# Normalising attention's output with features on partitions, its rows gathered by transfers

## The reference

```python
x = x + 0.5 * _L0_ffn_ref(_layernorm(x), ...)      # 8 experts, every token through each
x = x + _L0_attn_ref(_layernorm(x), ...)
x = x + 0.5 * _L0_ffn_ref(_layernorm(x), ...)
...
attn = jax.nn.softmax(scores, axis=-1)
ctx = jnp.einsum('bhqk,bhkd->bhqd', attn, v)
ctx = ctx.transpose(0, 2, 1, 3).reshape(b, t, D)
return ctx @ Wo.T + bo
```

## Time and profile before

| what | value |
|---|---|
| time, median of 3 runs | 778.74 us (778.41 to 781.88) |
| the profiled execution | 779.27 us |
| its span | 777.5 us |
| PE busy | 758.5 us, 98% |
| DVE busy | 476.2 us, 61% |
| POOL busy | 417.0 us, 54% |
| ACT busy | 348.5 us, 45% |
| DMA moved | 81.57 MB, mean 105 GB/s |

### The profile page before, as it was taken

How to read it: one execution, slowest core, us unless ns; L and a number is a source line. 1 busy time by engine, 2 the same in 40 slices (tenths; PEclk the granted TensorE clock), 3 DMA queues, 4 the chain that set the end, 5 groups by cost and what they waited for, 6 DMA issues and landing times.

```text
span 777.5 us, 14076 instructions
## 1 busy us (share of the span) xinstructions
PE 758.5 (98%) x4878; PEld 606.8 (78%) x4878; DVE 476.2 (61%) x1316; ACT 348.5 (45%) x657; POOL 417.0 (54%) x497
## 2 busy tenths in 40 slices
PE   6979999999999999999999999999999999999998
PEld 5868878976778777777778778677777778888887
DVE  6847754596657857787556667855657433473333
ACT  4455425525446544656344456453463453423222
POOL 4384867246654444844454853454554655655663
PEclk9999999999999999999999999999999999999999
DMA  9236423363213631323531222433222132223231
GB/s 304 84 103 192 163 74 105 103 201 96 70 55 92 177 101 62 103 62 106 161 117 48 82 86 89 140 97 109 77 89 83 48 104 82 82 67 124 84 117 58
DMA packets 60807, 81.57 MB, mean 105 GB/s; under 512 B 8384, under 2 KB 44608, under 8 KB 60736
## 3 DMA queue, kind: packets, MB, share of 16 engines
q1 hardware_dynamic: 58544, 80.36, 32.5%
q10 hardware_dynamic: 2192, 0.32, 0.2%
HBM read 67.78 MB, written 12.71 MB: 104 GB/s over the span
## 4 chain that ended last, share of the span: by engine, by line
PE 90%; DVE 6%; POOL 1%; issue 1%; DMA 1%; ACT 0%; DVEq 0%; POOLq 0%
PE ra L746 15%; PE ra L747 14%; PE ra L748 14%; PE dn L768 8%; PE dn L769 7%; PE dn L770 7%; PE ra L879 5%; PE ra L867 5%; PE ra L852 5%; PE ra L723 3%; PE ra L820 1%; PE ra L834 1%; PE ra L835 1%; PE ra L836 1%; PE ra L797 1%
## 5 line engine op out<-in xcount | busy, mean ns | idle before, releaser
L1357 POOL TENSOR_TENSOR hid<-hid,wb 128x512 f32<-128x512 f32 x124 | 161.5, 1303 | 183.0 <-DVE hid L1218 176.8
L746 PE MATMUL ra<-xt_hi,wgu_hi 128*128 128x512 f32 x512 | 226.5, 442 | 0.0
L1361 POOL TENSOR_TENSOR ht_lo<-hid,ht_hi 128x512 fp32r<-128x512 f32 x124 | 162.0, 1308 | 120.2 <-ACT ht_hi L997 119.8
L747 PE MATMUL ra<-xt_hi,wgu_lo 128*128 128x512 f32 x512 | 203.1, 397 | 0.0
L748 PE MATMUL ra<-xt_lo,wgu_hi 128*128 128x512 f32 x512 | 202.4, 395 | 0.0
L1269 DVE CUSTOM_DVE_ANT_0 junk<-ra,mask 128x128 bf16<-128x128 f32 (+3 forms) x256 | 121.0, 487 | 84.0 <-PE ra L852 81.3
L768 PE MATMUL dn<-wd,ht_hi 128*128 128x256 f32 x512 | 162.6, 318 | 2.7 <-POOL ht_lo L1361 2.7
L1210 DVE SCALAR_TENSOR_TENSOR hid<-hid,ra 128x512 f32<-128x512 f32 x125 | 85.7, 686 | 125.0 <-ACT hid L989 124.0
L769 PE MATMUL dn<-wd,ht_hi 128*128 128x256 f32 x512 | 144.9, 283 | 0.0
L770 PE MATMUL dn<-wd,ht_lo 128*128 128x256 f32 x512 | 144.5, 282 | 0.0
L997 ACT ACTIVATE ht_hi<-hid 128x512 fp32r<-128x512 f32 x124 | 78.0, 630 | 144.0 <-POOL hid L1357 119.4
(11 more groups left out here) (164 smaller groups left out, 859.4 us busy)
## 6 DMA issues: line engine op xcount, KB each, us to landing
wd<-wd_parts SPq DMA_DIRECT2D x56, 512.0 KB, 3.6
wb<-wts_rows SPq DMA_DIRECT2D x62, 256.0 KB, 3.7
qk_parts<-parts SPq DMA_DIRECT2D x32, 192.0 KB, 2.1
q_st<-qk_parts SPq DMA_DIRECT2D x96, 64.0 KB, 2.2
k_st<-qk_parts SPq DMA_DIRECT2D x96, 64.0 KB, 2.2
wd_parts<-wd SPq DMA_DIRECT2D x8, 512.0 KB, 3.0
x_res<-in_x SPq DMA_DIRECT2D x4, 512.0 KB, 8.5
stage<-in_Wg SPq DMA_DIRECT2D x8, 256.0 KB, 5.3
```

What stands on the lines that cost most here:

```text
L746: mm(b_, w_hi, xt_hi[q % 2][:, c, :], start=c == 0, stop=False)
L747: mm(b_, w_lo, xt_hi[q % 2][:, c, :], start=False, stop=False)
L1357: nc.gpsimd.tensor_tensor(tb, tb, wb[m % NWB][:, :], ALU.mult).then_inc(hw_done, 1)
L1361: nc.gpsimd.tensor_tensor(ht_lo[n % NHT][:, :], hidden(n)[:, :], f32(ht_hi[n % NHT][:, :]), ALU.subtract).then_inc(lo_done, 1)
```

## The change

`t1` and `t2` are gone, with their transposes and their banks. In their place:

- `cs` (SP): when ACT has copied a group to `cx`, eight DMAs (each 16 rows of 2 KB) carry the four heads' feature rows into `cn` and the sums' rows into a new tile `sums_of`, both now with features on partitions: half p of the features (groups 2p and 2p+1) fills 128 partitions by 512 queries.
- `nm` (DVE), once both groups of a half have landed: the reciprocal of `sums_of`, 128 x 512, in place, and the product with `cn`, 128 x 512.
- `ct` (ACT, then DVE): the rounded part and the rest of each half, now read from `cn` in SBUF and not from a PSUM bank.
- `wo` needs both halves of the features, so both `wo` of a batch wait for the second `ct` (`clo_done`).
- ACT's copy to `cx` waits for the `cs` of the group before; `cs` waits, at the first group of a half, for the `nm` that read `sums_of` last. `junk`, the scratch output of `max`, has two slots, not four.

```diff
-            put(meet[g + 1] + 1.3, ("t1", b, g))
+            put(meet[g + 1] + 1.0, ("cs", b, g))
...
-            put(meet[GR] + 2.4 + 0.2 * p, ("t2", b, p))
+            put(meet[2 * p + 2] + 2.0, ("nm", b, p))
+            put(meet[GR] + 2.2 + 0.2 * p, ("ct", b, p))
...
-            add("pe", ("t1", b, g), 0.45, ("act", "pv", b, g), ("pe", "t2", b - 1, 1) if g == 0 and b else None)
-            add("dve", ("t1", b, g), 0.7, ("pe", "t1", b, g))
+            add("sp", ("cs", b, g), 3.6, ("act", "pv", b, g), held, taken, kb=256)
...
-            add("pe", ("t2", b, m), 0.45, ("dve", "t1", b, GR - 1))
-            add("act", ("t2", b, m), 0.5, ("pe", "t2", b, m), ("pe", "v", b + 1, 1) if b + 1 < BATCH else None)
-            add("dve", ("t2", b, m), 0.6, ("act", "t2", b, m))
-            add("pe", ("wo", b, m), 1.42, ("dve", "t2", b, m))
+            add("dve", ("nm", b, m), 1.4, ("sp", "cs", b, 2 * m), ("sp", "cs", b, 2 * m + 1), port=True)
+            add("act", ("ct", b, m), 0.53, ("dve", "nm", b, m), ("pe", "v", b + 1, 1) if b + 1 < BATCH else ("pe", "wo", b - 1, 1))
+            add("dve", ("ct", b, m), 0.69, ("act", "ct", b, m), port=True)
+            add("pe", ("wo", b, m), 1.42, ("dve", "ct", b, 0), ("dve", "ct", b, 1))
...
-                    if kind == "t1":
-                        link(nc.vector.reciprocal(rec[:, :], heads[:, :, HD]))
...
+                    if kind == "nm":
+                        b, p = it[1:]
+                        dve.wait_ge(cs_ld, 128 * (b * GR + 2 * p + 2))
+                        link(nc.vector.reciprocal(sums_of[:, :], sums_of[:, :]))
+                        nc.vector.tensor_tensor(cn[:, p, :], cn[:, p, :], sums_of[:, :], ALU.mult).then_inc(nm_done, 1)
+                    if kind == "ct":
+                        b, p = it[1:]
+                        dve.wait_ge(chi_done, 2 * b + p + 1)
+                        nc.vector.tensor_tensor(ct_lo[:, p, :], cn[:, p, :], f32(ct_hi[:, p, :]),
+                                                ALU.subtract).then_inc(clo_done, 1)
...
+                    if kind == "cs":
+                        b, g = it[1:]
+                        p = g // 2
+                        sp.wait_ge(*emptied(("pv", b, g)))
+                        if g % 2 == 0 and b + p > 0:
+                            sp.wait_ge(nm_done, 2 * b + p)
+                        if g % 2 == 0 and b > 0:
+                            sp.wait_ge(clo_done, 2 * (b - 1) + p + 1)
+                        for h in range(GH):
+                            first = (g % 2 * GH + h) * HD
+                            for w, dst in enumerate((cn[:, p, :], sums_of[:, :])):
+                                sp.dma_start(dst[first:first + HD, :],
+                                             cx[(2 * h + w) * HD:(2 * h + w + 1) * HD, :]).then_inc(cs_ld, 16)
```

More of the change, by code:

```diff
@@ L202, in schedule @@
     return {it: t for t, it in at}
[L205 removed]
+RING = ("bias", "xt", "z", "wbp", "wt", "x", "qk", "v", "max", "mt", "exp", "pv", "wo")
 FREED_BY = {k: "act" for k in ("wbp", "wt", "v", "exp", "pv")} | {
[L207 removed]
+    k: "dve" for k in ("bias", "xt", "x", "z", "qk", "max", "mt", "wo")}
 FIRST = {"dve": {"t": -1.0, "h": -1.0, "max": 0.0, "sg": 0.0, "sd": 0.0, "stats": -0.2, "route": -0.5},
@@ L591, in build @@
         vf = sb("vf", [P, QT, H, 2 * HD])
-        junk = sb("junk", [P, NA, T], BF16)
+        junk = sb("junk", [P, NJUNK, T], BF16)
         mx = [sb(f"mx{i}", [P, GH * QT]) for i in range(2)]
@@ L607, in over @@
             return nc.alloc_sbuf_tensor_at(name, shape, dt, offset=at)
-        ct_hi = [over(f"ct_hi{i}", [P, KT, HT], F32R, x2_at + 2048 * i) for i in range(2)]
-        ct_lo = [over(f"ct_lo{i}", [P, KT, HT], F32R, x2_at + 4096 + 2048 * i) for i in range(2)]
+        ct_hi = over("ct_hi", [P, KT, T], F32R, x2_at)
+        ct_lo = over("ct_lo", [P, KT, T], F32R, x2_at + 4096)
         stage = [over(f"stage{i}", [P, KT, 3 * D], F32, probs_at + 6144 * i) for i in range(NSTAGE)]
@@ L881, in _ @@
                         last.then_inc(ra_full, 1)
-                    if kind == "t1":
-                        pe.wait_ge(*emptied(("pv",) + it[1:]))
-                        for i in range(QT):
-                            last = transpose(o[:, i * P:(i + 1) * P], cx[:, i * P:(i + 1) * P])
-                        last.then_inc(ra_full, 1)
-                    if kind == "t2":
-                        b, p = it[1:]
-                        pe.wait_ge(*emptied(("t1", b, GR - 1)))
-                        for i in range(2):
-                            for c in range(KT):
-                                last = transpose(o[:, (2 * c + i) * P:(2 * c + i + 1) * P],
-                                                 cn[:, 2 * p + i, c * P:(c + 1) * P])
-                        last.then_inc(ra_full, 1)
             @block.scalar
@@ L1051, in _ @@
                         if b + g > 0:
-                            act.wait_ge(ra_full, full(("t1", b, g - 1) if g else ("t1", b - 1, GR - 1)))
+                            act.wait_ge(cs_ld, 128 * (b * GR + g))
                         nc.scalar.activation(cx[:, :], o[:, :], ACT.Copy).then_inc(freed, 1)
-                    if kind == "t2":
+                    if kind == "ct":
                         b, p = it[1:]
-                        if p == 0 and b + 1 < BATCH:
-                            act.wait_ge(ra_full, full(("v", b + 1, 1)))
-                        nc.scalar.activation(ct_hi[p][:, :, :], o[:, :].rearrange("p (c t) -> p c t", c=KT),
-                                             ACT.Copy).then_inc(chi_done, 1)
+                        act.wait_ge(ra_full, full(("v", b + 1, 1) if b + 1 < BATCH else ("wo", b - 1, 1)))
+                        act.wait_ge(nm_done, 2 * b + p + 1)
+                        nc.scalar.activation(ct_hi[:, p, :], cn[:, p, :], ACT.Copy).then_inc(chi_done, 1)
             @block.vector
```

43 lines of the change are left out of this document (17 added, 26 removed).

## The result

| | before | after |
| --- | --- | --- |
| median, us | 779.81 | 788.00 |
| lowest to highest | 778.41 to 781.88 | 786.27 to 795.18 |
| ratio (95% interval) | | 1.012 (1.008 to 1.016) |
| the profiled execution | 779.27 | 786.27 |
| its span | 777.5 | 784.5 |

Seven runs of each; the change costs 8.2 us. The forecast was 784.0, in the range 770.5 to 794.0, and slower was held likeliest. For the profiled execution it was 784.5 against 786.27 measured.

The account below looks back on a forecast made before the run. PE's full queue was taken as the bound. For the profiled execution 779.27 - 9.3 (transposes removed) + 14.5 (new stalls) = 784.5 us, so 784.0 for the median, range 770.5 to 794.

Parts of the forecast that it names:

- The bound: PE's queue is full, busy 98% of the span; DVE work beyond its lead over PE is time lost.
- The removal: On PE, dropping `t1` and `t2` transposes saves 14 x 0.44 + 10 x 0.31 = 9.3 us.
- `nm`: 4.8 forecast: On DVE, each of eight `nm` takes 4.07 + 0.04 + 0.69 = 4.8 us, range 1.4 to 4.9.
- the first of two slopes: Reciprocal on DVE, from one and four elements in SBUF: 7.7 ns an element, 4.07 us for 512.
- The second slope: Reciprocal on DVE, from four to sixteen elements, source in PSUM: 6.3 ns an element, 3.4 us for 512.
- The stalls, place by place: PE waits at eight places behind `nm`, 0.6 to 3.2 us each, 14.5 us in all.
- SP: costed at nothing: On SP, 16 `cs` of up to 3.9 us each; weight loads and router rows behind them are early, so no cost.
- The last `wo`: Batch 3, second `nm`: no scores follow, PE comes to `wo` at 657.9 and waits 2.2 us.
- (a): Rival: the reciprocal on DVE is cheap, 0.7 us, `nm` 1.4, so 769.7 us; chance 0.14.
- (b): Rival: DVE's lump is long but mostly hidden, or the 3.4 us slope holds; 773 to 780 us; chance 0.28.
- (c): Rival: the lump spreads to POOL, ACT and SP, 8 to 12 us more in all, 793 us; chance 0.16.
- The forecast's case: The prediction's own outcome for the whole kernel, 780 to 788 us; chance 0.42.

Follow-up runs that it names:

- e1: Changed kernel with the reciprocal taken over 16 of the 512 columns only, so its result is not attention's: 771.77 us, ratio 0.989.
- e3: Changed kernel with the reciprocal over 16 columns and four DMAs in each `cs`, sums not carried: 771.13 us, ratio 0.989.
- e9: Kernel before with eleven more reciprocals of 1 to 512 elements at the end of DVE's list, read for their lengths; one execution took 789.34 us.
- e2: Changed kernel with four DMAs in each `cs` instead of eight, sums not carried, `sums_of` filled with ones once: 783.38 us, ratio 1.005.
- e11: Changed kernel with only the length of `cs` in the planner's table corrected, 3.6 to 4.9 us: 789.55 us, ratio 1.012.
- e5: Kernel before with eight added reciprocals of 128 x 512 that nothing reads, and `junk` with two slots: 790.71 us, ratio 1.012.
- e6: Order and banks of e4, but the whole reciprocal and product executed in one at the fourth piece: 785.34 us, ratio 1.006.
- e10: Changed kernel with only the length of `nm` in the planner's table corrected, 1.4 to 4.1 us: 772.34 us, ratio 0.991.
- e12: Changed kernel with `nm` in two pieces of 256 queries, 2.1 us each in the planner's table, and `cs` at 4.9: 770.17 us, ratio 0.987.
- e7: Changed kernel with both lengths in the planner's table corrected, `nm` 1.4 to 4.1 us and `cs` 3.6 to 4.9: 773.28 us, ratio 0.990.
- e8: Against e4: `nm` in eight pieces of 64 columns, 0.66 us each, and `cs` at 4.9 us in the planner's table: 782.1 us, ratio 1.002.
- e4: Changed kernel with `nm` in four pieces of 128 queries, separate planner's items of 1.2 us each: 771.98 us, ratio 0.990.

## Why the prediction was right, and where its terms were off

**The bound.** That PE's full queue is the kernel, and that a microsecond of DVE beyond its lead is lost, held: PE's instruction count is 96 lower, its idle time 13.4 us higher.

**The removal: 9.3 forecast, 7.7 to 8.0 measured** (e1 and e3). I took the larger of two prices (0.44) for 14 of the 24 places; the smaller (0.31) for all makes 7.4 and is nearer.

**`nm`: 4.8 forecast, 3.35 + 0.04 + 0.69 = 4.1 measured.** Too long because I trusted the first of two slopes, 7.7 ns from 155 and 178 ns. Three elements are too short a base: e9 has about the same there, 8 ns each from 1 to 4, and 6.25 from 4 to 16 and 6.26 over the whole range. The second slope, 6.3 over twelve elements, was right though its source is a PSUM bank. The Trainium skill, "VectorE: DVE Perf Modes", section "First, the fixed hardware budget", gave an estimate of 4.27 us by a repeat count of 8; the measurement, 3.35, decides against that reading of it. DVE rose by 22.2 us, not 28: eight times 0.7 less.

**The stalls, place by place** (us; measured is the idle time before the waiting PE instruction in after):

| place | forecast | measured |
| --- | --- | --- |
| batch 0, first | 0.6 | 0.91 |
| batch 0, second | 1.6 | 1.98 |
| batch 1, first | 3.2 | 2.42 |
| batch 1, second | 1.1 | none |
| batch 2, first | 2.9 | 1.86 |
| batch 2, second | 1.9 | 0.90 |
| batch 3, first | 1.0 | 0.65 |
| batch 3, last `wo` | 2.2 | 2.30 |
| sum | 14.5 | 11.0 |

Seven of eight are there, with the engines named. Corrected by the 0.7 us that `nm` was too long, batch 1's and 2's come to 2.5, 0.4, 2.2 and 1.2: close. At batch 1's first that is in part luck: I counted one DVE instruction behind the `nm`, but PE waited for two (0.6 us more), while after's list gave PE 2.95 us of work between the start of the `nm` and its wait, not the 1.62 + 0.7 = 2.32 that I took from before's (0.6 us less). In batch 0 the two are larger than forecast although `nm` is shorter: its `sums_of` had not landed. For the second, e2 shows it: where DVE didn't wait for the landing, PE's wait was 0.93 us. DVE sat 0.57 and 0.97 us in front of these, and 1.73 in batch 3 (after, DVE):

```profile
222.88 3.35 DVE L1267 RECIPROCAL sums_of<-sums_of 128x512 f32<-128x512 f32 x1 [0.57 <-DMA sums_of<-cx]
...
292.48 3.35 DVE L1267 RECIPROCAL sums_of<-sums_of 128x512 f32<-128x512 f32 x1 [0.97 <-DMA sums_of<-cx]
...
659.78 3.35 DVE L1267 RECIPROCAL sums_of<-sums_of 128x512 f32<-128x512 f32 x1 [1.73 <-DMA sums_of<-cx]
```

**SP: costed at nothing, and here the step failed.** I priced a `cs` by q_st's issue, 0.49 us for each DMA. Its own take 0.59 and start 0.63 us apart, so a `cs` is 5 us, not 3.9. And I had said that what stands behind it is early. In batch 0 it is not (after, SP, then PE):

```profile
265.87 0.52 SPq L1435 DMA_DIRECT2D cn<-cx  x1
...
270.23 0.59 SPq L1435 DMA_DIRECT2D sums_of<-cx  x1
270.92 2.87 SPq L1421 DMA_DIRECT2D q_st<-qk_parts  x6
```

```profile
279.89 0.22 PE L855 MATMUL ra<-k_st,q_st 96*128 96x128 bf16 x1 [1.41 <-DMA k_st<-qk_parts]
```

The score operands wait five us behind a `cs` and PE waits 1.4 for them. One of the six `k_st` issues behind them took 1.88 us where the others took 0.43, and either delay alone would have been too short for this wait. I had looked at weight loads and router rows behind `cs`, and not at score loads. e2 puts SP's share at up to 4.6 us with the long `nm`, e3 at 0.6 at most with a short one.

**The last `wo`: right by errors that cancel.** From `cx` done to the start of `wo` I had 13.0 us; it took 652.78 to 665.93, 13.15. The `cs` took 5.6 us, 1.7 more than forecast; the last landing came 1.4 us after its issue ended, 0.8 less than the 2.2; `nm` took 0.7 less. The 2.2 us of the earlier trace rows run from the start of an issue, and I had set them behind its end.

**The sum.** From 88.9 us to the end of the trace PE's work came 7.5 us later, where the forecast is 14.5 - 9.3 = 5.2. Measured: 11.0 + 0.3 (a second, short wait of L855 for `hid`) + 1.4 (`k_st`) + 0.4 (`probs`) - 7.8 = 5.3. Most of the 2.2 us that are missing stand in no idle time, and e1, whose PE has the same instructions in the same order, shows where they are. From 88.9 us on, after is 15.2 us longer than e1: 13.3 us are idle time and 1.9 lie between the starts of matmuls that the view counts as busy. Of these, 1.3 stand at eight of the waits, 0.16 at each: the matmul ahead of a stop counts as busy to its own end (0.39 us for one of 512 columns), where otherwise the next starts 0.23 us after it. A stop costs so much more than its idle row says.

**How much of the nearness is luck.** For the profiled execution 784.5 and 786.27 lie 1.8 us apart, but the terms erred by more: the removal was priced 1.5 us too high, the stalls 3.5 too high, SP's score loads and smaller waits (2.1) and what a stop costs beside its idle row (some 2) stood at nothing.

**From the profiled execution to the median: a term that I did not have.** The median came out 4.0 us above the forecast: 1.8 from above, and 2.2 because I took the median to lie 0.5 us below the profiled execution and it lies 1.7 above. The seven runs of after differ by 9 us, and their mean granted clock with them: 0.996 in the profiled one at 786.27 us, 0.993 at 786.53, 787.07 and 788.00, 0.987 at 791.20, 0.985 at 792.75, 0.981 at 795.18. The runs of before in the experiments stay at 0.993 to 0.997. Where the clock falls is to be seen in e11, at a wait of the same kind (PE in order of time, then stretches: length, PE busy, granted clock, DMA share, GB/s):

```profile
482.85 0.28 PE L774 MATMUL dn<-wd,ht_lo 128*128 128x256 f32 x1
...
485.52 0.36 PE L824 MATMUL ra<-x_hi,wa 128*128 128x256 f32 x1 [2.39 <-DVE hid L1207]
```

```profile
478.00:483.00 5.00, 5.00 (x34) 1.00 0.82 235
...
486.50:489.50 3.00, 3.00 (x15) 0.50 0.03 5
489.50:493.00 3.50, 3.50 (x14) 0.50 0.20 56
494.00:497.00 3.00, 3.00 (x20) 1.00 0.00 0
```

PE goes on after 2.39 us of idle time, full rate falls to half (2.4 to 1.2 GHz) from 486.4 to 493.2 us, and the 6.8 us of work at half rate cost 3.4. The same stands in e11 behind its wait of 2.34 us, in e2 behind those of 2.43 (half rate from 358.6 to 362.0) and 1.86, and in e5 and e6 behind waits of 1.95 and 2.02. In the profiled run of after, the waits of 2.42, 1.98 and 2.30 had no such stretch behind them. Nor does it take so long a wait: e10 and e12 have a stretch of 3.4 us behind a wait of 1.07 and 1.11 (after has the same wait, 1.11 us, and none), and e7 has one from 279.5 behind four waits of 0.11 to 0.46 us. So in some runs 1.7 or 3.4 us come on top of a stall's own length. That this is the 1.7 us between the profiled run and the median is likely by the mean clocks and not shown, since only the profiled run of after has a trace.

**The rivals.** (a) is out by the row of 3348 ns. (b) had the right slope, but its 8.9 us of stalls are 11.0. (c), that the cost spreads, is partly so: SP held score loads, and the mean clock was lower in some runs. No POOL wait grew. The forecast's case (780 to 788) holds the profiled run and the median's edge. What none of the four said is that most of these stalls were not the price of the long instruction at all, but of a number in a table: I read the `1.4` in the diff as the planner's matter and took after's order as given, and did not ask what an order made with 4.1 would do. It would not have changed this forecast, but it is what decides whether the idea is good.

## What to carry to other kernels

When an elementwise step moves to a layout in which each partition holds more elements, multiply its length by the elements in a partition, and look at what stands behind it in each in-order queue: here 16 times the elements made a 3.35 us lump. If a planner writes the order, give it the measured length of every new instruction before judging the change: one number (1.4 to 4.1) was worth 15.7 us, more than the 7.8 that the change could win. Splitting a long instruction in two or four gave as good a time (770.2 and 772.0 us, beside 772.3 and 773.3 for one piece at its true length, with intervals that overlap); in eight it took the gain away.

## What the runs showed of the hardware

- A reciprocal on DVE costs 6.26 ns an element in a partition on top of some 150 ns (1 to 512 elements, SBUF or PSUM). The product in the same place costs 1.04 ns an element on top of some 160 (226 ns for 64, 692 for 512).
- A DMA of 16 rows of 2 KB between two places in SBUF holds SP for 589 ns at the median, 0.63 us from start to start, where whole tiles of down weights (512 KB) take 326 ns at the median in the same list (319 to 525). From the end of its issue to its landing the last of a `cs` took 1.4 us.
- Small products with both operands in SBUF can take far longer than their median: 226 to 1341 ns for 64 elements in e8, 356 to 1424 for 128 in e4, yet 691 to 695 for 512 in after. The traces show when: each of the 23 products of e8 that took over 0.3 us started while a POOL instruction ran (22 of them one of POOL's products, some 1290 ns long) and ended 0.08 us after it; of after's eight, none started while POOL worked. In e7 two of the eight did, and one of them took 843 ns. The Trainium skill, "SBUF — State Buffer", section "Who interferes with whom", has the reason that fits: the second operand shares a read port with GpSimd, and whoever comes first keeps it. The rows of e8 agree. Ahead of each of after's eight products POOL had been idle for 1.0 to 4.4 us; that it had run out of work because of the 3.35 us before them is likely and wasn't tested.
- PE's granted clock fell to half for 3.4 or 6.8 us behind waits of 1.86 to 2.43 us in e2, e5, e6 and e11, behind one of 1.07 and 1.11 us in e10 and e12, and behind several of 0.11 to 0.46 us in e7, and not behind waits of 1.11 to 2.42 us in the profiled run of after.
- A stop of PE cost some 0.16 us beside the idle time in its row, at eight of the waits of after.
